# Lambda block, batch of 32: the last queries chunk loaded from ScalarE, and the first weight unit spread over six output tiles

## The reference, cut to what matters

```python
x = x + conv_block(groupnorm(x))                     # x: (32, 512, 64, 64) fp32
# conv_block(z):
h = relu(bn1(conv1x1(z, conv1_w)))                   # 512 -> 128 channels
q = bn(conv1x1(h, q_w))                              # 64 = 4 heads x 16
k = softmax(conv1x1(h, k_w), channels)               # 16
v = bn(conv1x1(h, v_w))                              # 32
pos = conv15x15(v, emb)                              # 16 x 32 maps, pad 7
content = einsum('bkm,bvm->bkv', k, v)
h = einsum('bhkn,bkv->bhvn', q, content) + einsum('bhkn,bkvn->bhvn', q, pos)
h = relu(bn2(h))
return relu(bn3(conv1x1(h, conv3_w)) + z)            # 128 -> 512 channels
```

## Time and profile before

| | |
|---|---|
| median of 3 runs | 4826.06 us (4821.62 to 4826.49) |
| the profiled execution, its own time | 4817.23 us |
| its span | 4815.5 us |
| TensorE busy | 4457.8 us, 93% |
| VectorE busy | 2796.9 us, 58% |
| ScalarE busy | 2346.0 us, 49% |
| POOL busy | 967.9 us, 20% |
| mean granted TensorE clock | 0.949 of full |
| DMA traffic | 1284.17 MB, mean 267 GB/s |

### The profile page before, as it was taken

One profiled execution on the slowest core, in us unless ns is written; L12 is line 12 of the kernel. 1 busy time (PEld: TensorE's weight loads), 2 busy tenths in 40 slices (PEclk: granted clock), 3 DMA queues, 4 the chain that ended last, 5 costly groups with the idle time before them and its releaser, 6 DMA issues.

```text
span 4815.5 us, 121009 instructions
## 1 busy us (share of the span) xinstructions
PE 4457.8 (93%) x49366; PEld 2717.4 (56%) x49366; DVE 2796.9 (58%) x4631; ACT 2346.0 (49%) x2880; POOL 967.9 (20%) x529
## 2 busy tenths in 40 slices
PE   4899999999999999999999999999999999999997
PEld 2555565655556655555555555555565556555555
DVE  3465555565655665656656556556566565566564
ACT  1455445554545454445544454544455444545453
POOL 0022211122201222202222112222122221112221
PEclk9899999999999999999999999999999999999998
DMA  3689778888778897788887788977888878889877
GB/s 96 214 278 308 239 265 279 275 296 277 249 272 266 282 309 250 254 274 288 281 291 243 265 266 276 307 251 254 272 292 281 288 245 275 270 273 305 263 248 250
DMA packets 537174, 1284.17 MB, mean 267 GB/s; under 512 B 43048, under 2 KB 225324, under 8 KB 528556
## 3 DMA queue, kind: packets, MB, share of 16 engines
q1 hardware_dynamic: 471276, 1017.22, 65.7%
q10 hardware_dynamic: 65472, 260.05, 14.7%
HBM read 844.79 MB, written 432.33 MB: 265 GB/s over the span
## 4 chain that ended last, share of the span: by engine, by line
PE 45%; SPq 18%; DMA 13%; issue 11%; DVE 6%; POOL 4%; ACT 2%; ACTq 0%; POOLq 0%; DVEq 0%
PE ring L527 16%; DMA X<-x_dram 11%; PE ring L653 10%; PE ring L508 7%; SPq L402 5%; PE ring L583 4%; SPq L360 4%; DVE st L884 3%; DMA q_parts<-region 3%; SPq L377 3%; POOL X L1189 2%; PE ring L534 2%; POOL region L1182 2%; SPq L378 2%; PE ring L539 2%
## 5 line engine op out<-in xcount | busy, mean ns | idle before, releaser
L702 ACT COPY region<-ring 126x1024 f32<-126x1024 f32 x1120 | 1102.9, 1016 | 948.0 <-PE ring L508 934.0
L583 PE MATMUL ring<-h,w3T 128*128 128x512 f32 x2048 | 937.7, 601 | 28.6 <-DVE X L1038 15.3
L653 PE MATMUL ring<-region,V 126*32 126x128 f32 x24576 | 889.2, 289 | 42.9 <-issue 42.7
L527 PE MATMUL ring<-X,w1e 128*128 128x512 f32 x2048 | 907.7, 596 | 3.2 <-DVE w1e L910 3.2
L508 PE MATMUL ring<-Qt,Ep 96*126 96x256 bf16 x5120 | 808.3, 298 | 103.9 <-DVE region L702 52.0
L653 PEld LDWEIGHTS ring<-region,V 126*32 126x32 f32 x24576 | 692.0, 116 | 223.3 <-issue 206.8
L702 DVE COPY region<-ring 126x1024 f32<-126x1024 f32 x416 | 507.5, 1220 | 496.6 <-PE ring L508 496.5
L508 PEld LDWEIGHTS ring<-Qt,Ep 96*126 96x126 bf16 x5120 | 598.9, 146 | 323.1 <-issue 139.4
L884 DVE BATCH_NORM_STATS2 st<-X 128x6 f32<-128x512 f32 x1024 | 624.8, 679 | 198.0 <-DMA X<-x_dram 197.9
L527 PEld LDWEIGHTS ring<-X,w1e 128*128 128x128 f32 x2048 | 384.5, 190 | 468.8 <-issue 465.5
L583 PEld LDWEIGHTS ring<-h,w3T 128*128 128x128 f32 x2048 | 370.0, 190 | 410.9 <-issue 371.5
(11 more groups left out here) (130 smaller groups left out, 3317.4 us busy)
## 6 DMA issues: line engine op xcount, KB each, us to landing
X<-x_dram SPq DMA_DIRECT2D x132, 2048.0 KB, 20.1
out_dram<-X SPq DMA_DIRECT2D x512, 512.0 KB, 8.0
X<-x_dram ACTq DMA_DIRECT2D x124, 2048.0 KB, 10.6
Qt<-q_parts SPq DMA_DIRECT2D x768, 128.0 KB, 3.1
V<-v_windows SPq DMA_DIRECT2D x96, 1024.0 KB, 10.5
lambda_sums<-S SPq DMA_DIRECT2D x64, 1024.0 KB, 5.0
h<-lambda_sums SPq DMA_DIRECT2D x256, 256.0 KB, 5.0
q_parts<-region SPq DMA_DIRECT2D x128, 256.0 KB, 4.2
```

The costliest lines, as they stand in the source:

```text
L527: last = nc.tensor.matmul(dst[:, hh * HALF:(hh + 1) * HALF], w1e[:, c, :], X[:, j, c, hh * HALF:(hh + 1) * HALF], start=(c == 0), stop=(c ...
L583: last = nc.tensor.matmul(dst[:, yb * HALF:(yb + 1) * HALF], w3T[:, t, :], src, start=True, stop=True)
L653: last = nc.tensor.matmul(bank_of(i)[c * DV:(c + 1) * DV, (g % 4) * P:(g % 4 + 1) * P], V[0:TROWS, VSLOT[t], xb, yb * DV:(yb + 1) * DV], W ...
L702: return engine_copy(dst, src)
```

## The change

Four edits. (1) The order of `MIX` and of the prologue: `w0.0` stands behind `o2.2`, `w0.1` behind `o2.3`, and then two lead items stand behind each of `o3.0` to `o3.3`, with the rests `r0` and `r1` behind `o3.1`, so that nothing follows the last pair. (2) Tiles `o2.2` and `o2.3` use ring 2 and 3, as `o3.*` do; VectorE moves slots 3 and 5 of unit 0, not 5 and 7. (3) ScalarE issues the six loads of q chunk 3, right behind its copy for `cl`; SP does not issue them, and SP's `load_v` stands behind three output stores, not four. (4) VectorE waits for all nine ReLUs of the round before `keep_for_output`.

```diff
-BY_DVE = {0: (5, 7), 1: (1, 3, 5), 2: (1, 3), 3: (3,), 4: (3,), 5: (1, 3, 5, 7)}
+BY_DVE = {0: (3, 5), 1: (1, 3, 5), 2: (1, 3), 3: (3,), 4: (3,), 5: (1, 3, 5, 7)}
...
 def lead_names():
-    return [f"w0.{s}" for s in range(NS)] + ["r0", "r1"]
+    return ["w0.0", "w0.1", "w0.2", "w0.3", "r0", "r1", "w0.4", "w0.5", "w0.6", "w0.7"]
...
-             "o1.0", "o1.1", "o1.2", "o1.3", "cl", "o2.0", "cp", "o2.1", "o2.2", "o2.3"]
-    lead = lead_names()
+             "o1.0", "o1.1", "o1.2", "o1.3", "cl", "o2.0", "cp", "o2.1", "o2.2", "w0.0", "o2.3", "w0.1"]
+    lead = lead_names()[2:]
     for t in range(4):
-        order += [f"o3.{t}", lead[t]]
-    return order + lead[4:]
+        order += [f"o3.{t}", lead[2 * t], lead[2 * t + 1]]
+    return order
...
-        elif name.startswith("o3"):
+        elif name.startswith("o3") or name in ("o2.2", "o2.3"):
             out[name] = 2 + int(name[3:]) % 2
...
                 load_q(b + 1, 2)
-                load_q(b + 1, 3)
                 store_v(b + 1)
-                for n in range(4, 8):
+                for n in range(4, 7):
                     store_out(b, n)
                 load_v(b + 1)
-                for n in range(8, 16):
+                for n in range(7, 16):
                     store_out(b, n)
...
+            def load_q(im, j):
+                act.wait_ge(q_out[j], im * 32 + 32)
+                for g, (a, _e) in enumerate(SPLIT):
+                    dst = bass.AP(Qt, g * (HEADS * N) + j * CHUNK, [[NG * HEADS * N, DK], [N, HEADS], [1, CHUNK]])
+                    act.dma_start(dst, qD[:, a, j * CHUNK:(j + 1) * CHUNK].rearrange("(h k) n -> k h n", k=DK))\
+                        .then_inc(q_in[j], 16)
...
                     elif name == "cl":
                         keys_out(AT_MIX, b + 1)
+                        load_q(b + 1, NCH - 1)
...
                 mixed(chain, MIX, AT_MIX, b, b + 1)
+                dve.wait_ge(half_relu, b * NPOOL + NPOOL)
                 keep_for_output(chain)
```

More of the change, by code:

```diff
@@ L321, in prior @@
             return out
-        LAST_LEAD = {0: "r0", 1: "r1"}
+        LAST_LEAD = {0: "w0.6", 1: "w0.7"}
         BEFORE_PRO = prior(PRO, AT_PRO, {})
```

## The result

The changed kernel takes 4847.1 us (median of 4 runs, 4836.41 to 4853.71) against 4823.84 us (median of 4, one more than above, 4815.37 to 4826.49) for the kernel before: a ratio of **1.0049**, 95% interval 1.0027 to 1.0072. It is slower by half a per cent, where 93 us faster were forecast, and outside the range. The profiled execution took 4836.41 us, 19.2 us more than that of before.

The account below looks back on a forecast made before the run. Each round was taken to have two gates, the tail's serial weight slots and the landing of X; the smaller of tensor advance plus 1.0 and X's advance gave 3.0 us, times 31 rounds 93 us: 4733 us, range 4690 to 4800.

Parts of the forecast that it names:

- part 1: Tail from `cl` to content: without the six slots behind the last tile, content begins at 2348.8, not 2350.70; 1.9 us a round.
- part 3: DMA queue: SP freed of six loads, so input X lands 2.2 to 3.8 us sooner; 3.0 taken.
- Rival B: Queries late, as ScalarE's loads share the engines with the windows' store; gain 1.2 us a round, 4789 us; chance 0.12.
- Part 2: Content and lambda start: if the granted clock holds, 3.2 us more, so TensorE is 5.1 us ahead in all.
- second gate: Lambda part: a slot VectorE moves only after X lands and 11 statistics; TensorE waits about 1 us a round for it.
- The sum: 31 rounds x 3.0 = 93 us, taken from the median of 4826.06: 4733 us.
- tensor advance: How much sooner TensorE reaches the lambda part: 1.9 us a round if the clock falls, 5.1 if it holds.
- X's advance: How much sooner the input X lands each round: 2.2 to 3.8 us, 3.0 taken.
- Rivals C and D: C: tail's gain given back whole at second gate, 4826 us, chance 0.05; D: clock falls sooner, 4947 us, chance 0.07.

Follow-up runs that it names:

- Run 3: Changed kernel, but SP begins the value windows' store only when query chunk 3 has landed; 4891.51 us, ratio 1.0151.
- run 1: Changed kernel with only the new order, rings and slot owners (edit 4 stays in); chunk 3's loads and the windows' store on SP as before; 4837.45 us, ratio 1.0040.
- run 5: Run 1 with `w0.0` and `w0.1` both behind `o2.3`; 4832.98 us, ratio 1.0041.
- run 6: Changed kernel, but ScalarE issues the windows' store early, behind the exponential of k3, and SP issues both last query chunks; 4840.54 us, ratio 1.0050.
- run 2: Kernel before with only the DMA change: chunk 3's loads on ScalarE, SP's window load behind three stores; 4911.82 us, ratio 1.0198.
- run 4: Changed kernel with queues exchanged: SP issues both last query chunks, ScalarE the windows' store beside them; 4867.66 us, ratio 1.0104.
- run 7: Run 6 with `w0.0` and `w0.1` both behind `o2.3`; 4771.14 us, ratio 0.9908.
- run 8: Run 6's placing of loads and windows' store, with the order, rings and slot owners of the kernel before; 4828.10 us, ratio 1.0034.
- run 11: Run 6 with `w0.0` and `w0.1` behind `o3.0` and four lead items behind `o3.2`; 4756.83 us, ratio 0.9871.
- run 12: Run 11 with VectorE moving slot w3.3 ahead of the second input chunk's three statistics in unit 2; 4776.80 us, ratio 0.9921.

## Why the prediction was wrong

**The step that failed** is in part 1: "the last begins 0.6 us before that and lands 3.2 us later, at 2332.0. TensorE would wait 1.3 us." That is 9.0 us after the `cl` matmuls; measured are 14.3, and `w0.0` waits 6.6 us a round. Both durations came from a stretch where one queue ran alone. Run 3 divides the miss: with ScalarE issuing and no windows' store beside the loads they land at 9.8 us, so 0.8 us were in the working and 4.5 us are the windows' store. Behind the step stands the sentence of part 3, "the loads are held by the issue and two issuers should overlap". They were not held by it to that degree: one issuer moved 94 to 119 packets a microsecond, two moved 111 and 113 in the changed kernel and at most 134 in run 3, and beside the windows the queries got 24 to 40. Low throughput (211 to 247 GB/s) was read as room. The Trainium skill's rule that the prediction weighed (DMA: Bandwidth & Descriptors, "Issuing engines are not separate DMA queues") says that a second issuing engine saves only issuing time. The trace agrees for the query loads: two issuers alone had them landed at 9.8 us (run 3), one at 10.0 (before).

**Rival B** had the mechanism with the wrong size. It let the queries run at half their rate, landing 10.8 us after `cl` (2333.8); beside the windows they ran at a quarter to a third. Its own numbers, 7 us where the forecast had 3.8, put the landing 3.2 us behind 2332.0, at 2335.2 or 12.2 us after `cl`, nearer to the measured 14.3.

**Part 1, the chain of the tail**, was nearly right given queries in time. From `w0.0` to content it had 16.8 us (2332.0 to 2348.8), and runs 1 and 5, with `w0.0` at 10.2 and 11.3 us, took 17.5 and 14.8 (in run 5 `o2.3`, some 1.8 us, stands ahead of `w0.0`). In the changed kernel it is 18.5, with one tile at the low clock.

**Part 2, the clock**, was right in its size and direction: content at 1.90 us in all 30 rounds of the changed kernel. The way there was partly luck. The reason given, idle time in small pieces, holds in run 5, which has no fall of the clock in the tail at all. In the changed kernel the clock does fall, in the new wait, and is back before content; `o2.3` takes 3.36 us in the mean and not 1.88, 1.5 us lost.

**Part 3, the second gate**, was right in kind and in size, but part of that is luck, since 3.0 was the middle of two bounds. X was taken to land 3.0 us sooner; it lands 2.8 us sooner (50.1 to 47.3), and VectorE's wait for it falls from 197.9 to 26.5 us. Runs 1, 3 and 5 show that it decides: whatever the tail gains with the input at 50 us is waited away. The reason given for the 3.0 us was half wrong: in run 3 SP is as free of the six issues, and X lands at 52.0 us. The gain came from windows and queries overlapping on the engines (done at 14.5 and not 17.5 us), and the same overlap is what delayed the queries by 4.3 us. The two terms of the sum were not independent, and the prediction added the good side of the overlap without its bad side.

**The sum.** The prediction's rule, the smaller of tensor advance plus 1.0 and X's advance, gives with the measured terms -5.3 + 3.2 + 1.0 = -1.1 us a round (an estimate); measured are -0.4. So the rule held and its term for the queries did not. 5.3 us lost in the tail, 5.0 won in the lambda part, 0.4 us more a round by the two rounded means; with the ends, 19.2 us in the profiled executions. **Rivals C and D** did not occur: the stores in front of X did not hold it, and the clock held over the last four tiles, but for a part of `o3.0` in 3 of the 30 rounds. It was low on `o2.3`.

**What stays open.** Why packets of the windows' store win over those of the queries, by 3 to 11 to one from one microsecond to the next, whichever queue carries which; and what limits the queries to some 110 packets a microsecond alone. Edit (4) was in run 1 and in all that build on it, and was not tried by itself. Also whether a placing exists with queries near 11 us and the input at 47. No run had both, and none kept the windows' store away from both the store and the loads of chunk 3 while it was early.

## What to carry to other kernels

When a transfer is moved to a second queue, price it beside what will now run with it, and not with the durations of a stretch in which it ran alone: here the same six loads landed 4.3 us later though they were issued sooner. If a stretch has two gates, a faster way to the first is worth only what the second can follow; run 5 gained 1.6 us in the tail and lost it all to the landing of the input, in a wait that also brought the clock down. Fit the order of the consumer to the landing as measured: the same DMA placing went from 1.0050 to 0.9871 when the first user moved from `o2.2` to `o3.0`.

## What the runs showed of the hardware that was not expected

Two queues moved hardly more query packets together (111 and 113 a microsecond, at most 134 in run 3) than one did (94 to 119), while a store of 1 KB packets took most of the engines from them on either queue. Its own rate beside them was 133 to 252; alone it ran at 197 to 207 on SP's queue (before, run 3), and on ScalarE's in run 6 it ran at 237 in a microsecond in which no 2 KB packet started, so query packets beside it are not what makes it fast. In three placings that overlap the two transfers (the changed kernel and run 2; run 4; runs 6 to 8, 11 and 12) the later of the two was done at 14.5 to 14.9 us, against 17.5 us one after the other; but in run 6 and those built on it that time comes from the late store of chunk 3, and not from full engines. And a DMA issue is not a fixed 0.6 us: ScalarE's six took 5.93 us once the windows' store was in the engines, and in run 7 SP's twelve took 11.30 us where they took 7.63 before. The windows' own four took 6.1 us on ScalarE in run 7, during which ScalarE did nothing else; on SP they took 5.8 us before (2330.51 to 2336.29), so that is not ScalarE's doing alone.
